# Finer load completion and read marks in a hybrid transformer layer on eight Trainium2 cores

## The reference, cut to what matters

```python
x = x + attn_a(layernorm(x), w_qkv, w_proj, b_proj)   # softmax(q k^T / 8) v over one head of 1024, rows swapped, then w_proj
x = x + ffn(layernorm(x), w_gate, w_up, w_down)        # (silu(x wg^T) * (x wu^T)) wd^T, hidden 3072, int32 weights / 127
x = x + attn_b(layernorm(x), proj_qk, proj_v, in_proj, out_proj)  # attention inside groups of 4, 8 heads of 128
x = x + ffn(layernorm(x), w_gate, w_up, w_down)        # the same ffn weights again
```

## Time and profile before

| | us |
|---|---|
| median of the 2 runs | 4878.47 |
| the two runs | 4798.11 and 4958.82 |
| the profiled execution, own time | 4799.2 |
| its span, slowest core (core 4) | 4797.7 |
| spans of the eight cores | 4786.2 to 4797.7 |

### The profile page before, as it was taken

How to read it: one execution, slowest core, us unless ns; L and a number is a source line. 1 busy time by engine, 2 the same in 40 slices (tenths; PEclk the granted TensorE clock), 3 DMA queues, 4 the chain that set the end, 5 groups by cost and what they waited for, 6 DMA issues and landing times.

```text
span 4797.7 us, 48198 instructions; the slowest of 8 cores (4786.2 to 4797.7 us)
## 1 busy us (share of the span) xinstructions
PE 3909.8 (81%) x17388; PEld 1670.6 (35%) x17728; DVE 900.7 (19%) x1568; ACT 1006.1 (21%) x1504; POOL 185.3 (4%) x340
## 2 busy tenths in 40 slices
PE   3799967999477776599983899959999666759999
PEld 1233323444232333144431333314444233314444
DVE  2200032221012222311112000132211222231111
ACT  1331212110023332211002421131100333231100
POOL 0000000000000000000000000000000000000000
PEclk8899987999787887699995999969999787769999
DMA  4200011222620000022243001102222200002233
GB/s 106 44 1 12 7 18 25 38 40 38 95 49 27 1 1 9 9 40 36 53 106 92 1 1 18 18 4 41 40 36 39 63 1 1 9 3 43 38 55 84
DMA packets 66098, 160.55 MB, mean 33 GB/s; under 512 B 6096, under 2 KB 6224, under 8 KB 61520
## 3 DMA queue, kind: packets, MB, share of 16 engines
q0 software_dynamic: 61056, 123.82, 16.5%
q1 hardware_dynamic: 4816, 33.63, 1.9%
HBM read 239.26 MB, written 25.19 MB: 55 GB/s over the span
## 4 chain that ended last, share of the span: by engine, by line
PE 79%; ACT 7%; DVE 6%; issue 4%; DMA 3%; another core or an unknown queue 1%; ACTq 0%; DVEq 0%; POOL 0%; POOLq 0%; SPq 0%
PE PS L95 54%; PE PS L678 14%; PE PS L515 5%; PE PS L556 2%; PE PS L268 2%; ACT SQ L262 2%; DVE XN L235 1%; DVE XN L288 1%; DMA XF<-x 1%; DMA AR<-wqk 1%; DMA AR<-wb 1%; DVE WB L982 1%; PE PS L335 1%; ACT WB L972 1%
## 5 line engine op out<-in xcount | busy, mean ns | idle before, releaser
L95 PE MATMUL PS<-XN,WB 128*128 128x512 bf16 x6018 | 1351.2, 385 | 75.8 <-DVE XN L288 67.1
L95 PEld LDWEIGHTS PS<-XN,WB 128*128 128x128 bf16 x6144 | 606.8, 99 | 820.4 <-issue 120.5
L678 PE MATMUL PS<-AR,WB 128*128 128x512 bf16 x3008 | 660.3, 379 | 7.8 <-DVE AR L627 4.5
L627 DVE SCALAR_TENSOR_TENSOR AR<-PS,SQ 128x512 bf16<-128x512 f32 x384 | 265.7, 692 | 1116.1 <-PE PS L95 1063.7
L621 ACT ACTIVATE SQ<-PS 128x512 bf16<-128x512 f32 x384 | 229.3, 597 | 1044.8 <-PE PS L95 1044.6
L678 PEld LDWEIGHTS PS<-AR,WB 128*128 128x128 bf16 x3072 | 300.3, 98 | 367.9 <-issue 6.3
L95 PE MATMUL PS<-AR,XN 128*128 128x512 bf16 x1756 | 417.0, 386 | 12.0 <-DMA AR<-wvT 7.5
L95 PE MATMUL PS<-AR 128*128 128x512 bf16 x1376 | 351.8, 414 | 19.1 <-DVE AR L288 12.8
L95 PE MATMUL PS<-XN,AR 128*128 128x512 bf16 x1242 | 308.6, 404 | 20.4 <-DVE AR L235 11.2
L515 PE MATMUL PS<-AR 128*128 128x512 bf16 x992 | 241.7, 383 | 22.5 <-DVE MISC L526 15.7
L95 PEld LDWEIGHTS PS<-AR,XN 128*128 128x128 bf16 x1792 | 166.7, 99 | 227.9 <-issue 52.3
(11 more groups left out here) (94 smaller groups left out, 1807.4 us busy)
## 6 DMA issues: line engine op xcount, KB each, us to landing
WB<-wg POOLq DMA_DIRECT2D x96, 256.0 KB, 3.8
WB<-wu POOLq DMA_DIRECT2D x96, 256.0 KB, 4.8
WB<-wdc POOLq DMA_DIRECT2D x96, 256.0 KB, 5.0
XF<-x SPq DMA_DIRECT2D x2, 8192.0 KB, 43.1
y<-XF SPq DMA_DIRECT2D x16, 1024.0 KB, 8.1
AR<-wb POOLq DMA_DIRECT2D x5, 2048.0 KB, 50.2
WB<-wpc POOLq DMA_DIRECT2D x32, 256.0 KB, 4.0
fw<-AR POOLq DMA_DIRECT2D x1, 6144.0 KB, 22.1
```

Of the source, the lines that this page charges most:

```text
L95: (lambda e: e.matmul(_o, _l, _r, start=_st, stop=_sp)))(),
L627: (lambda e: e.scalar_tensor_tensor(ar(S * _c + TT * _g, TT), bank(_bu), DEQ, _h, ALU.mult, ALU.mult)))(),
L678: (lambda e: e.matmul(bank(_b), wbs(_sl, 128 * (_c % 8), 128), ar(S * _c + TT * _g, TT), start=(_c == 0), stop=(_c == HHC - 1))))(),
```

## The change

Four edits, all in when something is waited for; no matmul, activation or byte of traffic is added or taken away.

1. `wqk` is loaded by eight DMAs of one chunk each (1 MiB of source) instead of two of four chunks, and every chunk of a wave waits for its own DMA.
2. In the down projection a TensorE semaphore increment stands behind every 4 hidden chunks (16 matmuls) instead of behind 24 (96 matmuls), and the read marks of `AR` slots are these. The marks of `WB` and PSUM stay at the end.
3. The load of `wbn1` moves behind those of `wb2` and `wb3`.
4. SP's DMAs alternate between two semaphores y0 and y1.

```diff
-        sname = "y"
+        sname = "y%d" % sch.sq
+        sch.sq = (sch.sq + 1) % 2
     w = list(waits) + [(sname, sch.cnt[sname])]
...
-                                    waits=(([wqld_a if oc < 4 else wqld_b]
-                                            if gi == 0 and oc in (0, 4) else []) +
+                                    waits=(([wq_dm[oc]] if gi == 0 else []) +
                                            (bank_w[gi] if oc == 0 else [])),
...
-                wqld_a = dma(sch, "gpsimd",
-                             lambda e: e.dma_start(
-                                 out=bass.AP(AR, 0, [[24 * S, 128], [2048, 4], [1, 2048]]),
-                                 in_=d_wqk[0:4].rearrange("c w p e -> p c w e")),
-                             wkeys=[("ar", s_) for s_ in range(4)])
-                wqld_b = dma(sch, "gpsimd",
-                             lambda e: e.dma_start(
-                                 out=bass.AP(AR, 8192, [[24 * S, 128], [2048, 4], [1, 2048]]),
-                                 in_=d_wqk[4:8].rearrange("c w p e -> p c w e")),
-                             wkeys=[("ar", s_) for s_ in range(4, 8)])
+                wq_dm = []
+                for oc in range(CH):
+                    wq_dm.append(dma(
+                        sch, "gpsimd",
+                        (lambda _oc=oc: (lambda e: e.dma_start(
+                            out=AR[:, 2048 * _oc:2048 * _oc + 2048],
+                            in_=d_wqk[_oc].rearrange("w p e -> p w e"))))(),
+                        wkeys=[("ar", oc // 1)] if False else [("ar", oc)]))
...
-                    rds = [("wb", pieces[i][0]) for i in range(3)] + \
-                        [("ar", s_) for s_ in range(24)]
+                    rds = [("wb", pieces[i][0]) for i in range(3)]
...
+                            mark_here = (c % 4 == 3 and g == NG - 1)
...
-                                   inc=("t" if (c == HHC - 1 and g == NG - 1) else None))
+                                   inc=("t" if mark_here else None))
+                        if c % 4 == 3:
+                            cm = ("t", sch.cnt["t"])
+                            for cc in range(c - 3, c + 1):
+                                sch.read(("ar", cc), cm)
...
-                ld_vn = dma(sch, "gpsimd",
-                            lambda e: e.dma_start(
-                                out=bass.AP(AR, 8192, [[24 * S, 128], [1024, CH], [1, 1024]]),
-                                in_=d_wbn1.rearrange("c p e -> p c e")),
-                            wkeys=[("ar", s_) for s_ in range(4, 8)])
...
-        sch.op("sync", None, waits=[("y", sch.cnt["y"])])
+        sch.op("sync", None, waits=[("y0", sch.cnt["y0"]), ("y1", sch.cnt["y1"])])
```

More of the change, by code:

```diff
@@ L44, in __init__ @@
         self.gq = 0
+        self.sq = 0
     def op(self, eng, fn, waits=(), inc=None, n=1):
@@ L170, in build @@
         sems = {k: ctx.enter_context(nc.semaphore("sem_" + k))
-                for k in ("t", "v", "s", "y", "g0", "g1", "g2", "g3")}
+                for k in ("t", "v", "s", "y0", "y1", "g0", "g1", "g2", "g3")}
         sch = Sched(sems)
@@ L722, in build @@
                             wkeys=[("ar", s_) for s_ in range(12, 16)])
+                ld_vn = dma(sch, "gpsimd",
+                            lambda e: e.dma_start(
+                                out=bass.AP(AR, 8192, [[24 * S, 128], [1024, CH], [1, 1024]]),
+                                in_=d_wbn1.rearrange("c p e -> p c e")),
+                            wkeys=[("ar", s_) for s_ in range(4, 8)])
                 ld_v2 = dma(sch, "gpsimd",
```

## The result

The changed kernel takes 0.9949 of the time of the kernel before, with a 95% interval of 0.9936 to 0.9961: 24 us less (19 to 31) of 4799. The profiled execution took 4770.9 us, against 4799.2.

What follows compares the result with a forecast made beforehand. The prediction took the kernel to be bound by TensorE's matmuls, which the change leaves alone. Gains of 4.3 + 19.2 + 3.0 + 2.8 = 29.3 us from 4799.2 gave 4770 us, range 4750 to 4855 (4763 to 4787 for an execution like the profiled one).

Steps and rivals of the forecast that it cites:

- (a): Start, to VectorE's first cast: fewer matmuls stand behind the last `wqk` chunk; 4.3 us gained.
- (c): Turn between the two sequences, where TensorE stands still until x lands: `fm` leaves earlier; 3.0 us gained.
- (b): Start of attn_b, first sequence, up to `fused_w`: its six weight loads leave earlier; 19.2 us gained.
- (d): End of `f1`, second sequence: `fw` leaves and lands earlier, so TensorE's projections start sooner; 2.8 us gained.
- Nothing else: Two semaphores for SP and 160 more increments in the down projection change nothing; 0 us each.
- Stage (e): First sequence, from the start of `fused_w` through attn_b to the end of `f2`; forecast difference 0.
- rival 3: Down projection: 160 new increments hold up TensorE, up to 61 us in all, time 4831; chance 0.03.
- Rival 1: Start: chunked `wqk` loads pay one by one, 4.2 us lost instead of 4.3 gained, time 4778; chance 0.10.
- rival 2: Start of attn_b: earlier loads don't shorten the chain as priced, 12 us gained, time 4777 or 4783; chance 0.08.

## Why the prediction was right or wrong

**The size, and against what.** I forecast 29.3 us less than the profiled execution and got 26.5 by the stages and 24 by the ratio, and the order of the terms held. That the profiled execution took 4770.9 for my 4770 is partly luck: (a) and (c) gave 3.2 us more than forecast, (b) and (d) 2.1 less, and 3.2 were lost in a stage that I had put at nothing.

**The step that failed in the framing.** The 4770 was worked out from an execution of 4799, but beside it stood a median of 4878.47, the middle of two executions 160 us apart; read against that median, 4770 says 2.2% faster, four times what the change does (0.5%). And "a measurement of this kernel tells about 2% from no change" was wrong: executions like the profiled one agree so well that 0.5% is clear, with an interval of 0.13% to either side. I should have forecast a small gain clear of noise, and not widened the range to 4855 for a mixture of runs.

**The step that failed in the mechanism: "Nothing else", 0 forecast, 3.2 us lost.** I looked for what the edits cost at the places that they touch. Stage (e), which no edit touches, costs 3 to 5 us in all kernels of the table with eight `wqk` loads, and takes back about half of what edit 1 gives in the changed kernel (3.2 of 7.0) and nearly all of it alone (5.3 of 6.1). It is shown that it belongs to edit 1, that 2.7 of the 3.2 us lie in the first layernorms of `f2` at a lower granted clock, and that an instruction of 0.24 us there brings nearly the same loss. The cause of the pause is open: delay, turn of the semaphores, early matmuls and longer lists of TensorE and POOL were each tried and each is not it. The rest of "nothing else" held: two semaphores for SP 0, the move of `wbn1` 0, increments 0 (rival 3).

**Term (a), mis-sized: 4.3 forecast, 7.0 measured.** "I price all of them there", at the lower clock, was wrong: the last six matmuls took 1.46 us and not 2.5, in groups that by then came about 3 us apart. That makes 5.5 us (7.1 from the last start of the wave to VectorE before, 1.6 after, means over the cores). The other 1.5 is the last chunk, which landed at 56.1 on the mean where the second half landed at 57.5; I had kept this only as an upper bound. Rival 1 fell: eight loads of 1 MiB landed no later than two of 4 MiB. What the Trainium skill's page "DMA: Bandwidth & Descriptors" (section "Rules for kernel authors") asks for, at least 1 MiB for each DMA, is just met here by the bytes of the source (512 KB as stored). The 2.0 us of fixed cost for each DMA that the same page gives (section "Anatomy of one DMA") are not seen here, where the next load is already queued.

**Term (b), right: 19.2 forecast, 18.0 measured.** The first load left at 1230.20 on core 1, 6.9 us behind the start of the last `ec` (1244.32 - 21.0 = 1223.3), of which 3.5 are the matmuls and 3.4 POOL's reaction: that is beyond my upper value of 3.0, and 2.1 more than the 1.3 that I took. So it left 17.1 us earlier against the end of `f1`, on every core, and not 19.2. The other 0.9 came from the loads: from the first issue to `fused_w` it took 80.6 us instead of 81.5 on the mean. The sum of the waits, 60.5 for 60 forecast, and the split with the long third wait came as written; rival 2 fell.

**Term (c), right: 3.0 forecast, 3.5 measured. Term (d), 2.8 forecast, 1.9 measured.** The mechanism of (d) was right, but I read it off the slowest core, where `fw` was late by 3 us. On the odd cores the stage already took 26.0 to 26.6 us before, against 27.4 to 29.2 on the even ones. On cores 1, 3 and 5 the layernorm was last anyway, and little was to be had.

## What to carry to other kernels

A completion that covers more than its waiter needs costs the difference: a mark behind every four of 24 hidden chunks cost nothing here and gave 18 us, and a wait for each loaded chunk gave 7 at the start, of which half was lost again elsewhere. Moving the loads earlier is the smaller half; moving the user that stands first in line behind the last load (the bias groups) gave 43 us more, because the matmuls that were already there then cover the loads. And before pricing a change from one core, compare the stages on all of them.

## What the runs showed of the hardware

- Six cast loads of 4 MiB of f32 go through one after another at 12.1 to 12.8 us each on the cores of five kernels read (before, after, and edits 1, 2 and 4 alone), whether they are issued early or late. With the bias groups in the order of their loads, the first lands at 1250.6 and the last at 1313.1 on core 4, most of it beside the matmuls of `fused_w`: 12.5 us each as well.
- Loads of 1 MiB of source queued behind each other lost nothing against loads of 4 MiB (last landing at 56.1 and 57.5 us).
- A load of 64 KB as stored, issued in the same instant as the 8 MiB load of x from the other queue, took 10.5 to 12.0 us to land (after, and edit 4 alone); where x left 1.4 us later, it took 3.2 to 4.0.
- In a stretch of 125 us with four layernorms, in which TensorE's clock falls and rises, all cores of a kernel agree within 0.06 us, and 0.24 us more on ScalarE made it 2.4 us longer, with a granted clock of 0.79 instead of 0.90 over the 48 matmuls behind the second layernorm.
- An edit at the start of the program brought such a loss 1900 us behind it, in every kernel that has it. In a kernel of 4800 us a term of 3 to 5 us can be of this sort, and only a run with the one edit alone tells it apart.
